# Layer 1 of a graph attention kernel: the sources' attention terms join the products as a 17th column

## The chip, the cores and the metric

The kernel runs on one core of one Trainium2 chip. The metric is the time of one execution on the device in microseconds. Before the change the median of 3 runs was 6350.81 us (6348.14 to 6351.27).

## The reference, cut

Four rounds of message passing over 200,000 edges between 6,250 nodes of 64 channels. Edges are sorted by destination. Three are attention layers (4 heads of 16 channels), the fourth is a linear one. What matters here is the attention layer:

```python
def _gatv2_layer(x, src, dst, Wl, Wr, a, b):
    xl = (x @ Wl).reshape(N, H, O)
    xr = (x @ Wr).reshape(N, H, O)
    s = jax.nn.leaky_relu(xl[src] + xr[dst], NEG_SLOPE)
    e = jnp.einsum('eho,ho->eh', s, a)
    m = jax.ops.segment_max(e, dst, num_segments=N)
    ex = jnp.exp(e - m[dst])
    denom = jax.ops.segment_sum(ex, dst, num_segments=N)
    alpha = ex / (denom[dst] + 1e-16)
    out = jax.ops.segment_sum(xl[src] * alpha[:, :, None], dst, num_segments=N)
    return out.reshape(N, H * O) + b
```

The kernel splits the leaky relu into 0.8 times max(s, 0) and 0.2 times s. The source's share of the second part, 0.2 (xl . a) for each head, is computed once per node and stored as 4 more columns of the table of sources (68 columns, TW). The destination's share is the same for all edges of a node and falls out of the softmax.

## The kernel before

The edges are laid over 128 partitions, 1568 edges in a row on each. A layer works through them in 98 turns of 16 edges a partition (G = 16), two turns to a round of the loop, each with its own buffer (k = 0 or 1). In each turn:

- The 16 source rows of a partition come into `xl[:, k]` (16 rows of 68) in two ways. GpSimd (POOL) issues 12 or 11 indirect DMAs from the table in memory (L552). The other 4 or 5 are fetched by the tensor engine (PE): products of a one-hot matrix with the table held in SBUF (L641), 28 matmuls for each share of 2 columns of edges and 42 for the one of 3. VectorE (DVE) picks the right one of 7 candidate rows with three predicated copies (L1245), and ScalarE (ACT) copies it into `xl` (`rows_copied`).
- DVE's `attention_turn`: the destination rows are spread along runs by a scan (L1284), then the sum `s` (L1307), the product with the positive part `lr` (L1309), the reduction over the 16 channels of a head (L1311), the addition of the source's term (L1312), the running maximum (a scan, L1314), two small operations on the arguments (L1316, L1317), a first select for the next turn, and the weighting `v_g` with the exponential `w_turn` (L1340). After it come the other selects, the one-hot matrix for a later step (layer 1 only, `build_one_hot`, L1233), the scan of the next destination rows, and the four scans of the weighted sums (L1287) with selects between them.
- ACT's `attention_turn`: a copy of the last destination row (`xr_carry`), the exponential `w_turn` (L874) as soon as the arguments are there, the marks for the next turn, the other factors (L858, L859), copies of fetched and of weighted rows, one widening of a one-hot matrix from bf16 (`widen_second`), and, once DVE's last scan of the sums is done (`s_sums`), the carry of the sums (`sums_carry`), the hand-out of the maximum and of the sums (`hand_out_max`, `hand_out`), and the other widening (`widen_first`). Nearly every copy of ACT is recorded with L766, the line of its helper, so groups are told apart by tiles.
- The sync engine (SP) stores the turn (`store_turn`, after `s_out`) and loads marks, indices and one-hot matrices or their codes.

Each engine works in its own written order and waits on semaphores. `done` and `steps_done` count DVE's dependent steps on `s_turn`, `K_TURN` = 5 a turn. `rows_of` gives the count of landed gathers that a turn needs. In layer 1 (`fresh` on ACT, `build` on DVE) the one-hot matrices are built; later layers load them again.

## Time and profile before

| | |
|---|---|
| median of 3 runs | 6350.81 us |
| the profiled execution | 6349.54 us, span 6347.7 us |
| mean granted clock of PE | 0.969 |
| PE busy | 5801.3 us (91%) |
| DVE busy | 5002.1 us (79%) |
| POOL busy | 4666.4 us (74%) |
| ACT busy | 4444.1 us (70%) |

Busy shares are averages over four layers with different limits, so they say little about one of them. Layer 1's loop lies between about 240 and 1670 us of the span, layers 2 and 3 behind it up to about 4750 us, and the linear layer follows. A timeline row has the start, the length, the engine, the line, the operation with its tiles and elements, and, where the engine was idle before it, for how long and what ended that. Neighbours on an engine may overlap by somewhat under 0.1 us, so a start minus the start before is what an instruction takes in a chain.

### The profile page before, as it was taken

The numbers are of one execution on the slowest core, as the hardware profiler recorded it, in microseconds if no ns is written. First come the engines' busy times: TensorE is split into PE (matmuls) and PEld (weight loads), VectorE is DVE, ScalarE is ACT, GpSimd is POOL, SyncE is SP. The second block draws the span as 40 slices with busy tenths as digits, with TensorE's granted clock in tenths as the row PEclk, the third lists the DMA queues.
The fourth block names the chain that finished last, engine by engine and source line by source line (L and its number), as shares of the span: only waits on it lengthen the run. The fifth ranks groups of instructions, "written<-read, shape, count | busy, mean of one in ns | idle before, by whom it ended". The sixth has DMA issues, their size and how long they took to land.

```text
span 6347.7 us, 100679 instructions
## 1 busy us (share of the span) xinstructions
PE 5801.3 (91%) x26479; PEld 4876.6 (77%) x26479; DVE 5002.1 (79%) x7708; ACT 4444.1 (70%) x6153; POOL 4666.4 (74%) x4884
## 2 busy tenths in 40 slices
PE   2899999999799999999969999999986999999996
PEld 1688787787578888888858888888864888888884
DVE  8699999999769999999958999999985444444443
ACT  1588888878468888888837888888874666666663
POOL 3777777777677777777767777777767777777775
PEclk9999999999799999999979999999997999999997
DMA  9677777777445555555535555555553444444442
GB/s 392 228 245 243 242 243 246 243 243 245 136 148 176 178 177 178 177 178 176 178 96 167 178 177 178 177 178 180 177 162 88 146 145 146 146 145 148 146 145 69
DMA packets 453003, 1153.13 MB, mean 182 GB/s; under 512 B 158796, under 2 KB 224832, under 8 KB 416876
## 3 DMA queue, kind: packets, MB, share of 16 engines
q1 hardware_dynamic: 281624, 927.58, 40.5%
q0 software_dynamic: 156944, 173.32, 14.7%
q10 hardware_dynamic: 14404, 51.92, 2.1%
q14 instruction: 24, 0.20, 0.0%
q8 instruction: 7, 0.11, 0.0%
HBM read 754.04 MB, written 398.35 MB: 182 GB/s over the span
## 4 chain that ended last, share of the span: by engine, by line
POOL 41%; issue 20%; PE 13%; DVE 11%; ACT 8%; DMA 3%; SPq 2%; DVEq 1%; POOLq 0%; ACTq 0%
POOL sb_xl L552 36%; PE pG L641 12%; ACT sb_v_in L766 3%; DVE pG L1245 3%; POOL sb_hot_f L552 3%; DVE sb_s_run L1287 2%; ACT sb_hot L766 2%; ACT sb_turn_out L766 2%; DMA sb_xl<-xl_table,sb_idx 2%; POOL marks L556 1%; SPq L364 1%; DVE sb_e_in L1311 1%; DVE sb_lr L1309 1%; DVE sb_s L1307 1%; ACT pB L766 1%
## 5 line engine op out<-in xcount | busy, mean ns | idle before, releaser
L641 PE MATMUL pG<-sb_xl_parts,sb_hot 128*128 128x476 f32 (+1 forms) x25074 | 5507.8, 378 | 221.0 <-ACT sb_xl L766 121.5
L641 PEld LDWEIGHTS pG<-sb_xl_parts,sb_hot 128*128 128x128 f32 x25074 | 4683.2, 189 | 1041.7 <-issue 422.8
L552 POOL DMA_INDIRECT sb_xl<-xl_table,sb_idx x4481 | 4271.2, 953 | 1381.0 <-issue 1352.7
L766 ACT ACTIVATE sb_hot<-sb_wide 128x1792 fp32r<-128x1792 bf16 (+1 forms) x796 | 1485.8, 1880 | 267.1 <-DMA sb_wide<-hots 227.0
L1245 DVE COPY_PREDICATED pG<-sb_pick_turn,pG 128x272 f32<-128x272 int32 (+9 forms) x2388 | 1110.6, 465 | 551.5 <-PE pG L641 455.6
L1287 DVE TENSOR_TENSOR_SCAN sb_s_run<-pB,sb_v_in 128x272 f32<-128x272 f32 (+3 forms) x1470 | 1095.9, 773 | 220.6 <-ACT sb_v_in L999 219.2
L766 ACT ACTIVATE sb_turn_out<-sb_s_run 128x1088 f32<-128x1088 f32 (+2 forms) x399 | 831.9, 2086 | 6.0 <-DVE sb_s_run L1287 6.0
L1284 DVE TENSOR_TENSOR_SCAN pB<-sb_same_c,pB 128x1024 f32<-128x1024 f32 x294 | 672.1, 2286 | 0.2
L766 ACT ACTIVATE sb_xl<-pG 128x136 f32<-128x136 f32 (+4 forms) x838 | 251.6, 303 | 502.6 <-DVE pG L1245 381.9
L766 ACT ACTIVATE sb_v_in<-sb_v_g 128x1024 f32<-128x1024 f32 x291 | 600.7, 2064 | 0.0
L1307 DVE TENSOR_TENSOR sb_s<-sb_xl,pB 128x1024 f32<-128x1024 f32 x294 | 354.5, 1206 | 143.5 <-DMA sb_xl<-xl_table,sb_idx 141.3
L1311 DVE TENSOR_REDUCE sb_e_in<-sb_lr 128x64 f32<-128x1024 f32 x294 | 359.2, 1222 | 10.1
L1309 DVE SCALAR_TENSOR_TENSOR sb_lr<-sb_s,pB 128x1024 f32<-128x1024 f32 x294 | 359.0, 1221 | 10.1
L766 ACT ACTIVATE sb_same_c<-sb_same 128x960 f32 (+1 forms) x294 | 305.7, 1040 | 70.0 <-DVEq L1226 61.9
L1340 DVE TENSOR_TENSOR sb_v_g<-sb_xl,pB 128x1024 f32<-128x1024 f32 x291 | 353.0, 1213 | 0.0
L766 ACT ACTIVATE pB<-sb_mark 128x960 f32<-128x960 f32 x294 | 287.0, 976 | 39.0 <-DMA sb_mark<-marks 21.1
L999 ACT ACTIVATE sb_v_in<-sb_s 128x1024 f32<-128x1024 f32 x97 | 198.9, 2051 | 129.4 <-DVE sb_s L1539 128.1
L766 ACT ACTIVATE sb_v_in<-sb_s_run 128x68 f32<-128x68 f32 (+1 forms) x389 | 126.3, 325 | 189.3 <-DVE sb_s_run L1287 189.3
L874 ACT ACTIVATE pB<-sb_wf_arg 128x64 f32<-128x64 f32 x291 | 65.6, 226 | 245.5 <-DVE sb_wf_arg L1317 242.8
L1539 DVE TENSOR_TENSOR sb_s<-sb_xl,pB 128x1024 f32<-128x1024 f32 x98 | 119.7, 1221 | 138.9 <-DMA sb_xl<-xl_table,sb_idx 119.3
L858 ACT ACTIVATE sb_v_in<-sb_wf_arg 128x64 f32<-128x64 f32 x294 | 75.6, 257 | 168.9 <-DVE sb_v_g L1340 168.9
L556 POOL DMA_INDIRECT marks<-sb_XR,sb_first_edge x147 | 147.0, 1000 | 62.1 <-issue 62.1
(261 smaller groups left out, 2309.4 us busy)
## 6 DMA issues: line engine op xcount, KB each, us to landing
state_rows<-sb_turn_out SPq DMA_DIRECT2D x294, 576.0 KB
sb_wide<-hots SPq DMA_DIRECT2D x149, 1120.0 KB
sb_mark<-marks SPq DMA_DIRECT2D x294, 512.0 KB
sb_wide<-hots SPq DMA_DIRECT2D x149, 896.0 KB
sb_xl<-xl_table,sb_idx POOLq DMA_INDIRECT x4481
sb_wide<-codes SPq DMA_DIRECT2D x50, 1120.0 KB
hots<-sb_wide SPq DMA_DIRECT2D x50, 1120.0 KB, 4.3
marks<-sb_hot_f SPq DMA_DIRECT2D x32, 1568.0 KB
```

The source lines that it names most:

```text
L552: return pool.indirect_dma_start(out=dst, out_offset=None, in_=table, in_offset=bass.IndirectOffsetOnAxis(ap=index, axis=0))
L556: return pool.indirect_dma_start(out=table, out_offset=bass.IndirectOffsetOnAxis(ap=index, axis=0), in_=src, in_offset=None)
L641: product = pe.matmul(pG[:, bank + a - lo, 0:GB * n], hot[k][:, m, a * P:(a + 1) * P], rows[:, :, 0:n], start=(m == 0 and part == 0), stop ...
L766: return act.activation(out, in_, ACT.Copy)
L999: act.activation(v_lin[:, :, 1:G1], s[:].rearrange("p g c -> p c g"), ACT.Relu).then_inc(s_lin_relu, 1)
L1245: return dve.copy_predicated(rows[:, :, 0:n], over(pick_turn[:, k, stage, lo:hi], n), rows[:, :, at:at + n])
L1284: dve.tensor_tensor_scan(xr_flat, same_c[:].rearrange(flat3), xr_flat, 0.0, ALU.mult, ALU.add).then_inc(s_xr, 1)
L1287: return dve.tensor_tensor_scan(s_run[:, lo:hi, :].rearrange(flat3), factors[:, 0:(hi - lo) * G1], v_in[:, lo:hi, :].rearrange(flat3), 0.0 ...
L1307: tt(s[:], xl[:, k, :, 0:C], xr.rearrange("p c g -> p g c"), ALU.add).then_inc(s_added, 1)
L1309: done(dve.scalar_tensor_tensor(out=lr[:], in0=s[:], scalar=0.0, in1=blocks(a_turn, G), op0=ALU.max, op1=ALU.mult)); steps_done()
L1311: done(red(e_turn.rearrange("p h g -> p g h"), lr[:].rearrange("p g (h o) -> p g h o", h=H), AX.X, ALU.add)); steps_done()
L1340: tt(v_g[:].rearrange("p g (h o) -> p g h o", h=H), xl_heads, weights, ALU.mult).then_inc(s_used[k], 1)
```

## The change

In layer 1 the product tile becomes 16 x 4 x 17 values for each partition. The products fill columns 0 to 15 of each head (in all layers), and in layer 1 ACT copies the source's attention term, `xl[:, k, :, C:TW]`, into column 16. DVE's reduction then runs over 17 columns, and its addition L1312 is left out there. ACT copies the terms of a turn ahead, between `hand_out_max` and `hand_out` of the turn before, after it has waited for the gathers and the fetched rows of that turn; the terms of turn 0 are copied ahead of the loop. DVE waits for a new semaphore `s_terms` before the reduction.

```diff
-        lr = sb("lr", [P, G, C])
+        lr_sums = sb("lr", [P, G, H, O + 1])
+        lr = lr_sums[:, :, :, 0:O]
...
+            def attention_terms(landed, copied, k):
+
+                act.wait_ge(s_xl[k], landed)
+                for q in range(2):
+                    act.wait_ge(s_rows[q], copied)
+                copy(lr_sums[:, :, :, O], xl[:, k, :, C:TW]).then_inc(s_terms, 1)
+
...
                     hand_out_max(use * 16, k)
+                    if fresh:
+                        attention_terms(rows_of(l, i + k, 1 - k), selected, 1 - k)
                     hand_out(turn_all + 1, k)
...
                 spread_same(l * TURNS + 1, 1)
+                if fresh:
+                    attention_terms(rows_of(l, 0, 0), l * STEPS + 3, 0)
                 widen_step(4, 0)
...
-                done(dve.scalar_tensor_tensor(out=lr[:], in0=s[:], scalar=0.0, in1=blocks(a_turn, G), op0=ALU.max, op1=ALU.mult)); steps_done()
+                s_heads = s[:].rearrange("p g (h o) -> p g h o", h=H)
+                a_heads = blocks(a_turn.rearrange("p (h o) -> p h o", h=H), G)
+                done(dve.scalar_tensor_tensor(out=lr, in0=s_heads, scalar=0.0, in1=a_heads, op0=ALU.max, op1=ALU.mult)); steps_done()
                 e_turn = e_in[:, 0, :, 1:G1]
-                done(red(e_turn.rearrange("p h g -> p g h"), lr[:].rearrange("p g (h o) -> p g h o", h=H), AX.X, ALU.add)); steps_done()
-                done(tt(e_turn, e_turn, xl[:, k, :, C:TW].rearrange("p g h -> p h g"), ALU.add)); steps_done()
+                e_heads = e_turn.rearrange("p h g -> p g h")
+                if terms:
+                    dve.wait_ge(s_terms, turn_all + 1)
+                    red(e_heads, lr_sums[:, :, :, :], AX.X, ALU.add).then_inc(s_turn, 2)
+                    steps[0] += 2
+                    steps_done()
+                else:
+                    done(red(e_heads, lr, AX.X, ALU.add)); steps_done()
+                    done(tt(e_turn, e_turn, xl[:, k, :, C:TW].rearrange("p g h -> p h g"), ALU.add)); steps_done()
```

`terms` is set in all turns of layer 1 and in no other layer. The prologue's temporary in the same tile is only given its new shape.

## Rows read from the trace of the kernel before

**Rows 1.** Windows, mid layer 1: busy us (xinstructions) of PE, PEld, DVE, ACT, POOL; clock, DMA, GB/s.

```profile
500.00:750.00 250.00, 237.93 (x1075) 200.02 (x1074) 246.46 (x374) 201.38 (x289) 190.30 (x196) 1.00 0.76 244
```

**Rows 2.** Waits of 2000 to 3000 us, layer 2: total us, times, longest.

```profile
DVE sb_s L1307 <- DMA sb_xl<-xl_table,sb_idx: 56.4, 36, 1.8
```

**Rows 3.** DVE's groups, 400 to 1500 us: busy us, mean ns, idle us before.

```profile
L1311 DVE TENSOR_REDUCE sb_e_in<-sb_lr 128x64 f32<-128x1024 f32 x75 | 91.7, 1222 | 2.6
...
L1307 DVE TENSOR_TENSOR sb_s<-sb_xl,pB 128x1024 f32<-128x1024 f32 x74 | 88.0, 1189 | 0.0
...
L1312 DVE TENSOR_TENSOR sb_e_in<-sb_e_in,sb_xl 128x64 f32<-128x64 f32 x75 | 20.6, 275 | 2.6
...
L1316 DVE TENSOR_TENSOR sb_e_in<-sb_m_run,sb_neg_h 128x64 f32<-128x64 f32 x75 | 16.9, 225 | 2.6
```

**Rows 4.** Timeline of DVE, an odd turn of layer 1.

```profile
868.16 1.19 DVE L1307 TENSOR_TENSOR sb_s<-sb_xl,pB 128x1024 f32<-128x1024 f32 x1
...
870.63 1.22 DVE L1311 TENSOR_REDUCE sb_e_in<-sb_lr 128x64 f32<-128x1024 f32 x1
871.89 0.27 DVE L1312 TENSOR_TENSOR sb_e_in<-sb_e_in,sb_xl 128x64 f32<-128x64 f32 x1
872.20 0.30 DVE L1314 TENSOR_TENSOR_SCAN sb_m_run<-sb_neg_h,sb_e_in 128x68 f32<-128x68 f32 x1
...
872.79 0.34 DVE L1317 TENSOR_TENSOR sb_wf_arg<-sb_e_in,sb_m_run 128x128 f32<-128x128 f32 x1
873.13 0.59 DVE L1245 COPY_PREDICATED pG<-sb_pick_turn,pG 128x408 f32<-128x408 int32 x1
873.63 1.21 DVE L1340 TENSOR_TENSOR sb_v_g<-sb_xl,pB 128x1024 f32<-128x1024 f32 x1
...
897.60 1.19 DVE L1307 TENSOR_TENSOR sb_s<-sb_xl,pB 128x1024 f32<-128x1024 f32 x1
```

**Rows 5.** Timeline of ACT in the same turn.

```profile
868.26 0.33 ACT L766 ACTIVATE sb_v_in<-sb_s_run 128x68 f32<-128x68 f32 x1 [0.95 <-DVE sb_s_run L1287]
868.49 0.30 ACT L766 ACTIVATE sb_turn_out<-sb_m_run 128x64 f32<-128x64 f32 x1
868.70 2.17 ACT L766 ACTIVATE sb_turn_out<-sb_s_run 128x1088 f32<-128x1088 f32 x1
870.77 2.44 ACT L766 ACTIVATE sb_hot<-sb_wide 128x2688 fp32r<-128x2688 bf16 x1
873.11 0.21 ACT L766 ACTIVATE sb_xr_carry<-pB 128x64 f32<-128x64 f32 x1
873.21 0.23 ACT L874 ACTIVATE pB<-sb_wf_arg 128x64 f32<-128x64 f32 x1
873.50 0.98 ACT L766 ACTIVATE pB<-sb_mark 128x960 f32<-128x960 f32 x1
874.87 0.26 ACT L858 ACTIVATE sb_v_in<-sb_wf_arg 128x64 f32<-128x64 f32 x1 [0.39 <-DVE sb_v_g L1340]
```

**Rows 6.** Timeline of ACT, the exponential of the even turn behind it.

```profile
887.55 0.23 ACT L874 ACTIVATE pB<-sb_wf_arg 128x64 f32<-128x64 f32 x1 [0.61 <-DVE sb_wf_arg L1317]
```

**Rows 7.** Timeline of ACT and DVE in the last turn of layer 1.

```profile
1666.09 0.23 ACT L874 ACTIVATE pG<-sb_wf_arg 128x64 f32<-128x64 f32 x1 [2.31 <-DVE sb_wf_arg L1317]
...
1666.35 1.98 DVE L1323 TENSOR_TENSOR sb_v_in<-sb_xl,pG 128x1024 f32<-128x1024 f32 x1 [0.29 <-ACT pG L874]
```

**Rows 8.** Timeline of POOL and DVE beside the one-hot build.

```profile
875.31 1.59 POOL L552 DMA_INDIRECT sb_xl<-xl_table,sb_idx  x1 [0.30 <-issue]
...
876.03 0.75 DVE L1233 TENSOR_SCALAR sb_wide<-sb_wide,sb_code_no 128x2048 bf16<-128x2048 int16 x1
...
877.21 0.94 POOL L552 DMA_INDIRECT sb_xl<-xl_table,sb_idx  x1 [0.30 <-issue]
```

**Rows 9.** Timeline of PE in the same turn.

```profile
876.59 21.82 PE L641 MATMUL pG<-sb_xl_parts,sb_hot 128*128 128x476 f32 x98 [1.20 <-ACT sb_xl L766]
```

**Rows 10.** Timeline of DVE near the end of layer 1.

```profile
1657.46 0.59 DVE L1245 COPY_PREDICATED pG<-sb_pick_turn,pG 128x408 f32<-128x408 int32 x1 [0.58 <-PE pG L641]
```

More of the change, by code:

```diff
@@ L216, in build @@
         pe_src = s[0:STEPS].rearrange("p g c -> p (g c)")[:, 0:ECX].bitcast(I32)
-        pe_tmp = lr[0:STEPS].rearrange("p g c -> p (g c)")[:, 0:ECX]
+        pe_tmp = lr_sums[0:STEPS].rearrange("p g h o -> p (g h o)")[:, 0:ECX]
         out_flat = turn_out[:].rearrange("p k g r -> p (k g r)")
@@ L298, in build @@
         s_e_carried = sem("max_carried")
+        s_terms = sem("attention_terms_in")
         s_sums, s_out, s_stored = sem("sums_scanned"), sem("turn_out_ready"), two("turn_stored")
@@ L1295, in linear_sums, with attention_turn @@
                 scan_sums(same_part, LIN_SUMS[-2], LIN_SUMS[-1]).then_inc(s_sums, 1)
-            def attention_turn(l, i, k, last=False, build=False):
+            def attention_turn(l, i, k, last=False, build=False, terms=False):
                 use = l * PAIRS + i
@@ L1393, in attention_layer @@
                     for k in range(2):
-                        attention_turn(l, i, k, build=build)
-                attention_turn(l, PAIRS - 2, 0, build=build)
-                attention_turn(l, PAIRS - 2, 1)
-                attention_turn(l, PAIRS - 1, 0)
-                attention_turn(l, PAIRS - 1, 1, last=True)
+                        attention_turn(l, i, k, build=build, terms=build)
+                attention_turn(l, PAIRS - 2, 0, build=build, terms=build)
+                attention_turn(l, PAIRS - 2, 1, terms=build)
+                attention_turn(l, PAIRS - 1, 0, terms=build)
+                attention_turn(l, PAIRS - 1, 1, last=True, terms=build)
                 dve.wait_ge(s_sums, (l + 1) * TURNS)
```

## The prediction, made before the change was built

> **What bounds the kernel now.** I read the busy time by stretches first, then the groups of instructions of layer 1's loop, then the timelines of VectorE (DVE) and ScalarE (ACT) over one pair of turns side by side. In a stretch in the middle of layer 1 DVE is busy 246.46 of 250 us [rows 1], and the sum of sources and destinations, which starts each turn, waited for nothing in 74 turns (idle 0.0) [rows 3]. So DVE sets the pace there: two turns take 29.44 us (868.16 to 897.60, the starts of two sums of the same parity) [rows 4]. In layers 2 and 3 the same sum waits for the gathers of sb_xl, 36 times in 1000 us and up to 1.8 us each [rows 2]: they pace that loop, and DVE's length is hidden there. The change touches the work of layer 1 alone, except for the pitch of sb_lr, below.
>
> The two turns of a pair are not alike, and this decides the case. Call a turn odd when ACT has just widened the large share of the one-hot matrix (2688 columns, 2.44 us), and even when it was the small one. In the odd turn at 868.16 follow both engines from one event, the end of the last scan of the sums. DVE goes sum, product, reduction (870.63), the addition (871.89), the running maximum (872.20), arguments (872.79), a select (873.13), and at 873.63 the weighting sb_v_g, which needs ACT's exponential [rows 4]. ACT goes carry (868.26), maximum (868.49), hand-out (868.70), widening (870.77), xr_carry (873.11), exponential, 873.21 to 873.44 [rows 5]. In this chain ACT has no gap at all: its idle time of 0.95 us is before the carry, and the exponential follows xr_carry at once. From 873.44 to the weighting's start are 0.19 us; of these 0.03 go to the hand-over (ACT's exponential ends at 1666.32, DVE's product starts at 1666.35 [rows 7]). So ACT is only 0.16 us ahead of being the later of the two. In the even turn ACT waited 0.61 us for the arguments before the same exponential [rows 6]; there it has room.
>
> **Part 1: the addition goes.** It takes 275 ns [rows 3], and from its start to the start of the running maximum it is 0.31 us (871.89 to 872.20) [rows 4]. That is what goes, the gap that follows each dependent step included.
>
> **Part 2: the reduction reads 17 columns.** 1088 elements in place of 1024. Between an operation of 64 elements (225 ns) and the one of 1024 (1222 ns) an element costs 997/960 = 1.04 ns [rows 3], so 64 more cost 0.07 us. DVE's own chain becomes shorter by 0.31 - 0.07 = 0.24 us in each turn. Its additional wait for the terms costs nothing: the copy comes 0.44 us after ACT's carry starts and the reduction 2.47 us after the sum starts [rows 4, 5], and the running maximum, which already waits for two semaphores (`steps_done` and `s_e_carried`), shows the same 0.04 us gap (872.16 to 872.20) as the addition that waits for one (871.85 to 871.89) [rows 4].
>
> **Part 3: ACT's copy.** No row shows it: 64 elements in runs of four, read from SBUF at a pitch of 68 and written at a pitch of 17. It stands between the maximum's copy and the hand-out, so it pushes back the hand-out, the widening, xr_carry and the exponential. What matters is its step, from its start to the start of what follows. From below: the exponential of 64 elements into sb_v_in takes 0.26 us, less the 0.09 by which neighbours overlap (868.49 + 0.30 against 868.70) is 0.17; I take 0.16 to 0.17. The copy of the maximum, also 64 elements and read at a pitch of 17, has a step of 0.21, and the carry, scattered on both sides, 0.23 [rows 5]. From above: the copy has three waits and a register to work out, and the copy of the marks starts 0.29 us after the exponential before it (873.21 to 873.50), although that lasts 0.23, for it has such waits in front [rows 5]; so 0.30. A step below nothing is excluded, since ACT works in order. I take 0.22, nearest to the two scattered copies, with 0.16 and 0.30 as ends.
> The wait for the gathers that is put in front of the copy would hold up the hand-out, its store, the widening for TensorE (PE) and the exponential. It is the wait that DVE's next sum has too, and that sum starts at 868.16, before the carry, never having waited for gathers [rows 3]; so it costs nothing. ScalarE's widening ends near 873.2 and PE begins the following share at 876.59, after a wait for another copy [rows 9]; 0.22 us more are hidden there by some 3 us. SP's queue gets its store 0.22 us later in a period of 14 us, and ACT waits for that store only two turns later. If that cover went, each 0.1 us would cost 0.1 us a turn.
> The Trainium skill's page "ScalarE: Activation LUTs", section "What ACT_TABLE_LOAD costs", gives 186 ns plus 0.833 ns an element for such an ACTIVATE, and 93 ns of overlap of neighbours. An estimate by that page is 239 ns and a step of 0.15 us. The trace has 0.30 us and a step of 0.21 for 64 scattered elements [rows 5], so here the row speaks against it.
>
> **The sum.** Even turns: ACT's exponential could run 0.61 us before it did; with the copy 0.39, and DVE's arguments come 0.24 earlier. DVE still comes last, so the whole 0.24 is won. Odd turns: DVE would be ready for the weighting 0.24 us earlier, but ACT's exponential comes 0.22 later and had 0.16 to spare: the weighting starts 0.22 - 0.16 = 0.06 us later than now. The gain turns into a wait for ACT. Of 49 even turns the one next to the layer's end wins nothing, because DVE waits 0.58 us for PE behind it [rows 10]: 48 x 0.24 = 11.5 us won. Of 49 odd turns the last one has no widening before it and wins 0.24; the other 48 lose 48 x 0.06 = 2.9. Together 11.5 + 0.2 - 2.9 = 8.8 us won. The profiled execution took 6349.54 us, so 6340.7; the median of the runs shown lies 1.3 us above that execution, which makes 6342.0 us. With a step of 0.16 odd turns neither win nor lose: 11.7 us, 6339.1. With 0.30 they lose 48 x 0.14 = 6.7: 5.0 us won, 6345.8.
> What else could come last at this pace: GpSimd (POOL). Its gathers follow each other at 1.24 us [rows 8] and there are 23 in a pair, 28.5 us, plus one that took 1.59 in place of 0.94, 29.2. That looks almost like a bound at today's 29.44, but the long one (875.31 to 876.90) ends 0.12 us after the one-hot build that DVE runs from 876.03 to 876.78 [rows 8]: it is held by that build and shrinks when POOL comes later relative to DVE. Its 0.65 us are room, more than the 0.18 us by which the pair shortens. PE idles 1.20 us a pair [rows 9].
>
> **The rivals.** (a) *Both turns win.* Then 97 x 0.24 = 23.3 us, 6327.5. It needs the weighting at 873.39, while ACT's exponential already ends at 873.44 before the change [rows 4, 5]; only a chain of ACT that I misread allows it. 4%.
> (b) *A cheap copy.* ACT's exponential into PSUM, 64 elements too, takes 0.23 us [rows 5], a step of 0.14. With that odd turns win 0.02: 12.7 us, 6338.1, and a little less or 0.02 more slack is over 0.2%. That contiguous row speaks for it, both scattered ones against. 14%. By the Trainium skill's page "ScalarE: Activation LUTs", section "What ACT_TABLE_LOAD costs", it would be this case.
> (c) *ACT becomes the bound of both turns: slower.* Beyond a step of 0.37 (0.61 less 0.24) even turns wait for ACT as well, and a pair changes by (step - 0.16) + (step - 0.61). That is nothing at a step of 0.385; from 0.52 it is slower by over 0.2%; at 0.60 it is +0.43 a pair, 21 us, 6372. For it: three waits on one instruction, in a queue that has no gap. Against it: 0.29 is the longest such step in the rows. 8%.
> (d) *The pitch of 17 slows DVE.* DVE's product into sb_v_in, all of it scattered, took 1.98 us, against 1.21 for the same product into rows [rows 4, 7]. sb_lr is now written in runs of 16, and read so in layers 2 and 3. If a run costs one element more, 64 x 1.04 = 0.07 us, even turns win 0.17, odd ones don't notice, and it is 5.5 us won, 6345.3; if it cost the whole 0.77 us in each turn it would be some 50 us slower. The 225 ns step reads runs of 16 at a pitch of 17 and shows nothing of it. 6%, of which 1 slower.
> (e) *POOL falls into a build twice in a pair*, another 0.65 us: its period would be 28.5 + 1.3 = 29.8, DVE would come to wait for gathers, and 49 pairs would take 49 x 0.36 = 18 us more than now, 6368. It holds only if the new phase keeps hitting. 4%.
>
> **How the numbers follow.** The forecast has 64%: 6342.0, of its own range 6339 to 6346. A measurement of this kernel can tell some 0.2% (12.7 us) from no change, that is below 6338.1 or above 6363.5. Faster: (a), and two thirds of (b), 13%. Slower: most of (c), half of (e), the worst of (d), 9%. Within: 78%. The range holds 8 in 10 from 6336.5 ((b), with the 1.5 us by which runs scatter) to 6350 (mild (d) and the first half of (c)).
>
> **What would show it.** In the profile after: no 64-element addition in layer 1; a reduction of 1088 elements at 1.29 us; a copy from sb_xl to sb_lr on ACT, with its step; in odd turns a wait of the weighting for ACT's exponential of some 0.2 to 0.3 us, in even turns none, and an idle time before the even exponential of some 0.15 us; a pair of 29.26 us; layers 2 and 3 unchanged. I am wrong if the odd turn's weighting doesn't wait, if the copy's step lies outside 0.14 to 0.30, or if sb_lr's product takes other than 1.22 us.

## The result and the profile after

The changed kernel takes 6358.1 us (median of 20 runs) against 6349.8 us for the kernel before (20 runs): a ratio of 1.0014, 95% interval 1.0008 to 1.0020, or 8.3 us more. The forecast was 6342.0 us, 7.8 us less, and the time lies outside its range. That is 0.13%, less than the 0.2% that the prediction took as the least change one can tell, but the interval excludes no change at all, and the direction is the opposite of the forecast's. One of the 20 runs (6850.9 us, with a mean granted clock of 0.803 in place of 0.969) was a slow one and is left out of the ratio.

| | before | after |
|---|---|---|
| profiled execution (span) | 6349.54 (6347.7) us | 6369.94 (6368.1) us |
| a pair of turns in layer 1, from sum to sum | 29.45 us | 29.65 us |
| odd turn, even turn | 14.38, 15.06 us | 14.38, 15.26 us |
| layer 1, first sum to last | 1426.3 us | 1434.9 us |
| layers 2, 3 and 4 | 1391.6, 1390.8, 1395.1 us | 1395.8, 1394.8, 1397.6 us |

A pair of turns is one round of the loop. The profiled execution of after is 11.8 us above its own median. Its gathers (the indirect DMAs that POOL issues) lasted 0.947 us in place of 0.944; some 3360 gathers in layers 2 to 4 by 0.003 us are 10 us, and these three layers together are 10.7 us longer. That is a matter of this execution and not of the change: e2 below has the same pitch of sb_lr there, and gathers of 0.944 us, and its layers 2 to 4 take 1390.9, 1391.4 and 1394.6 us. The profiled executions of e1 and e3 are of the same kind as after's, that of g8 is not, and its layer 1 is as long (1434.4 us). What makes the gathers of an execution longer isn't known. The timed difference of 8.3 us is layer 1's 8.6.

Windows in the middle of layer 1, after, answering to [rows 1]:

```profile
500.00:750.00 250.00, 236.73 (x1067) 198.76 (x1066) 244.72 (x353) 202.00 (x304) 190.75 (x194) 1.00 0.76 242
```

VectorE (DVE) is busy for 1.7 us less of 250, yet a pair takes 0.20 us longer. Its groups of 400 to 1500 us, after, answering to [rows 3] (busy us, mean ns, idle us before):

```profile
L1329 DVE TENSOR_REDUCE sb_e_in<-sb_lr 128x64 f32<-128x1088 f32 x75 | 96.6, 1288 | 6.7
...
L1324 DVE SCALAR_TENSOR_TENSOR sb_lr<-sb_s,pB 128x1024 f32<-128x1024 f32 x75 | 91.6, 1222 | 2.6
...
L1320 DVE TENSOR_TENSOR sb_s<-sb_xl,pB 128x1024 f32<-128x1024 f32 x74 | 88.0, 1190 | 0.0
...
L1246 DVE TENSOR_SCALAR sb_wide<-sb_wide,sb_code_no 128x2560 bf16<-128x2560 int16 x37 | 39.7, 1072 | 0.0
...
L1246 DVE TENSOR_SCALAR sb_wide<-sb_wide,sb_code_no 128x1920 bf16<-128x1920 int16 x37 | 34.5, 932 | 0.0
```

The same two builds of the one-hot matrix in the same view of the kernel before:

```profile
L1233 DVE TENSOR_SCALAR sb_wide<-sb_wide,sb_code_no 128x2560 bf16<-128x2560 int16 x37 | 33.0, 892 | 0.0
...
L1233 DVE TENSOR_SCALAR sb_wide<-sb_wide,sb_code_no 128x1920 bf16<-128x1920 int16 x37 | 26.4, 712 | 0.0
```

The addition is gone, the reduction takes 1288 ns, the product still 1222. But two instructions that the change doesn't touch grew by 0.18 and 0.22 us in each pair: the two builds of the even turn. Here they are in the timeline of DVE, after, a pair of turns from 872.11 us (odd) and 886.49 us (even), answering to [rows 4]:

```profile
872.11 1.19 DVE L1320 TENSOR_TENSOR sb_s<-sb_xl,pB 128x1024 f32<-128x1024 f32 x1
...
877.57 1.22 DVE L1362 TENSOR_TENSOR sb_v_g<-sb_xl,pB 128x1024 f32<-128x1024 f32 x1
...
879.99 0.75 DVE L1246 TENSOR_SCALAR sb_wide<-sb_wide,sb_code_no 128x2048 bf16<-128x2048 int16 x1
...
886.49 1.19 DVE L1320 TENSOR_TENSOR sb_s<-sb_xl,pB 128x1024 f32<-128x1024 f32 x1
887.71 1.22 DVE L1324 SCALAR_TENSOR_TENSOR sb_lr<-sb_s,pB 128x1024 f32<-128x1024 f32 x1
889.02 1.29 DVE L1329 TENSOR_REDUCE sb_e_in<-sb_lr 128x64 f32<-128x1088 f32 x1
890.35 0.30 DVE L1336 TENSOR_TENSOR_SCAN sb_m_run<-sb_neg_h,sb_e_in 128x68 f32<-128x68 f32 x1
...
891.99 1.21 DVE L1362 TENSOR_TENSOR sb_v_g<-sb_xl,pB 128x1024 f32<-128x1024 f32 x1
...
893.61 0.92 DVE L1246 TENSOR_SCALAR sb_wide<-sb_wide,sb_code_no 128x1920 bf16<-128x1920 int16 x1
...
894.91 1.07 DVE L1246 TENSOR_SCALAR sb_wide<-sb_wide,sb_code_no 128x2560 bf16<-128x2560 int16 x1
```

ScalarE (ACT) in the same pair, answering to [rows 5, 6]; in brackets its idle time and what ended it:

```profile
872.65 0.30 ACT L768 ACTIVATE sb_lr<-sb_xl 128x64 f32<-128x64 f32 x1
872.80 2.17 ACT L768 ACTIVATE sb_turn_out<-sb_s_run 128x1088 f32<-128x1088 f32 x1
...
877.32 0.22 ACT L883 ACTIVATE pB<-sb_wf_arg 128x64 f32<-128x64 f32 x1
...
891.27 0.23 ACT L883 ACTIVATE pB<-sb_wf_arg 128x64 f32<-128x64 f32 x1 [0.20 <-DVE sb_wf_arg L1339]
```

GpSimd (POOL), answering to [rows 8]:

```profile
878.74 1.05 POOL L554 DMA_INDIRECT sb_xl<-xl_table,sb_idx  x1 [0.30 <-issue]
880.09 1.46 POOL L554 DMA_INDIRECT sb_xl<-xl_table,sb_idx  x1 [0.30 <-issue]
...
893.10 0.95 POOL L554 DMA_INDIRECT sb_xl<-xl_table,sb_idx  x1 [0.30 <-issue]
894.35 0.98 POOL L554 DMA_INDIRECT sb_xl<-xl_table,sb_idx  x1 [0.30 <-issue]
895.64 1.16 POOL L554 DMA_INDIRECT sb_xl<-xl_table,sb_idx  x1 [0.30 <-issue]
```

Read the even turn against these. Its weighting starts 5.50 us after its sum (before: 888.23 - 882.54 = 5.69), so 0.19 us are won, as meant. Then both builds start about half a microsecond into a gather (893.61 against 893.10, 894.91 against 894.35) and last 0.92 and 1.07 us. That gives 0.21 and 0.18 us back, and the turn ends 0.20 us later than before. In the odd turn the weighting starts 5.46 us after the sum, against 5.47: it waits for ACT's exponential, which ends at 877.54.

In the kernel before, the even turn's builds met the gathers at other points. DVE's two builds and POOL's gathers beside them:

```profile
889.85 0.71 DVE L1233 TENSOR_SCALAR sb_wide<-sb_wide,sb_code_no 128x1920 bf16<-128x1920 int16 x1
...
890.95 0.89 DVE L1233 TENSOR_SCALAR sb_wide<-sb_wide,sb_code_no 128x2560 bf16<-128x2560 int16 x1
```

```profile
888.44 0.94 POOL L552 DMA_INDIRECT sb_xl<-xl_table,sb_idx  x1 [0.30 <-issue]
889.69 0.98 POOL L552 DMA_INDIRECT sb_xl<-xl_table,sb_idx  x1 [0.30 <-DVE sb_v_g L1340]
890.98 0.98 POOL L552 DMA_INDIRECT sb_xl<-xl_table,sb_idx  x1 [0.30 <-issue]
```

They started 0.16 and 1.26 us after the start of the latest gather, and kept their length. The first two even turns of layer 1 in the changed kernel still take 14.87 and 14.90 us, with short builds; from the third on they take 15.27. How the loop gets from the one to the other is shown under e4.

### The profile page after: what moved, and what is told of

Same layout as the page of the kernel before. It is cut to its first block, busy times and chain, and to the rows that moved or that the text cites. A ratio compares the mean times of both kernels' runs of the same rounds, so it can differ in the third digit from the quotient of the medians.

```text
span 6368.1 us, 100875 instructions
## 1 busy us (share of the span) xinstructions
PE 5809.6 (91%) x26479; PEld 4875.3 (77%) x26479; DVE 5000.5 (79%) x7610; ACT 4461.9 (70%) x6251; POOL 4687.0 (74%) x4884
## 4 chain that ended last, share of the span: by engine, by line
POOL 48%; issue 23%; DVE 10%; ACT 8%; DMA 4%; PE 3%; SPq 2%; DVEq 1%; POOLq 0%; ACTq 0%
POOL sb_xl L554 43%; ACT sb_v_in L768 3%; DVE pG L1258 3%; POOL sb_hot_f L554 3%; PE pG L643 3%; DMA sb_xl<-xl_table,sb_idx 2%; ACT sb_hot L768 2%; DVE sb_s_run L1300 2%; ACT sb_turn_out L768 2%; POOL marks L558 1%; SPq L366 1%; DVE sb_lr L1324 1%; DMA sb_idx<-src_edges 1%; DVE sb_s L1320 1%; DVE sb_e_in L1329 1%
## 5 line engine op out<-in xcount | busy, mean ns | idle before, releaser
L1333 DVE TENSOR_REDUCE sb_e_in<-sb_lr 128x64 f32<-128x1024 f32 x196 | 239.4, 1222 | 6.7
```

The costliest lines, as they stand in the source:

```text
L1333: done(red(e_heads, lr, AX.X, ALU.add)); steps_done()
```

## The experiments

The theory formed from the two traces: a build on DVE and a gather on POOL hold each other up, and the shortened turn moved the builds onto the bad part of the gathers. The rivals: ACT's copy on the path of the odd turn's exponential, the pitch of 17, and the additional wait.

### The halves of the change, and more work added

**e1_after_again** is the changed kernel once more, beside the next three.

> The changed kernel once more, as the measure for the others of this group. Meeting theory (the shorter even turn moves the two builds of the one-hot matrix in it to where a gather of GpSimd is at work, and both engines then hold each other up; the loop settles there): a pair of turns of 29.6 us, in even turns builds of 0.93 and 1.07 us in place of 0.71 and 0.89, some 8 us slower than before. Rival (the 12 us that the first profile of the changed kernel has outside layer 1 belong to the change): layers 2 to 4 again 4, 4 and 3 us longer than before and a time near 6370.

Measured: 6356.85 us against 6348.15 (33 runs of the kernel before), 1.0011 (1.0002 to 1.0020); a pair of 29.64 us, the even turn's builds 0.93 and 1.07 us. It repeats.

**e2_copy_alone**: ACT copies the terms, DVE computes as before.

```diff
-                    dve.wait_ge(s_terms, turn_all + 1)
-                    red(e_heads, lr_sums[:, :, :, :], AX.X, ALU.add).then_inc(s_turn, 2)
...
+                    done(red(e_heads, lr, AX.X, ALU.add)); steps_done()
+                    done(tt(e_turn, e_turn, xl[:, k, :, C:TW].rearrange("p g h -> p h g"), ALU.add)); steps_done()
```

> Only ScalarE's part: it copies the terms into column 16 with all its waits, while VectorE sums 16 columns and adds the terms itself as before. Meeting theory: VectorE's turns keep their length (the copy's step of 0.15 us fits into ScalarE's 0.16 us of room in odd turns), so the builds stay where they were: a pair of 29.45 us and the time of before within 2 us. Rival (ScalarE's later hand-out and exponentials cost the time): 8 us slower than before, as the whole change is.

Measured: 6350.64 us, 1.0001 (0.9992 to 1.0010), and a pair of 29.45 us. Its builds, 400 to 1500 us:

```profile
L1246 DVE TENSOR_SCALAR sb_wide<-sb_wide,sb_code_no 128x2560 bf16<-128x2560 int16 x37 | 33.0, 893 | 0.0
...
L1246 DVE TENSOR_SCALAR sb_wide<-sb_wide,sb_code_no 128x1920 bf16<-128x1920 int16 x37 | 26.4, 713 | 0.0
```

The copy and the pitch of 17 cost nothing by themselves. DVE's shortening is needed for the loss.

**e3_dve_alone**: 17 columns on DVE, no copy on ACT. Column 16 is set to zero once, so the sources' terms are left out of the sums.

```diff
-                    if fresh:
-                        attention_terms(rows_of(l, i + k, 1 - k), selected, 1 - k)
...
-                    dve.wait_ge(s_terms, turn_all + 1)
...
+                if build:
+                    dve.memset(lr_sums[:, :, :, O], 0.0)
```

> Only VectorE's part: it reduces 17 columns and has no addition, column 16 is zeroed once ahead of the loop, ScalarE copies nothing and VectorE doesn't wait for it. The sources' attention terms are left out of layer 1. Meeting theory: even turns are 0.24 us shorter up to the weighting, so the builds meet the gathers as in the changed kernel, and it is no faster than before (6350 to 6362) with builds of over 0.9 us in even turns. Rival (ScalarE's part eats the gain): 18 to 22 us faster than before, 6328 to 6332, builds of 0.71 and 0.89 us.

Measured: 6349.12 us, 1.0000 (0.9991 to 1.0009). Without the copy the odd turn is 14.22 us, 0.16 shorter than in the changed kernel: that is the copy's step of 0.15 on ACT's path. The even turn is 15.27 us, as long as in the changed kernel, with the same long builds:

```profile
L1242 DVE TENSOR_SCALAR sb_wide<-sb_wide,sb_code_no 128x2560 bf16<-128x2560 int16 x37 | 39.6, 1071 | 0.0
...
L1242 DVE TENSOR_SCALAR sb_wide<-sb_wide,sb_code_no 128x1920 bf16<-128x1920 int16 x37 | 33.9, 917 | 0.0
```

By the prediction's sum this kernel should have won 0.24 us in each even turn and, with no copy on ACT, its 0.16 us of room in each odd one, 19 us in all. The odd turns won their 0.16 and the even turns lost 0.20, so nothing was won, with ACT's copy out of the case. This also settles the gap of 0.09 us ahead of the long reduction (888.93 to 889.02 in the trace of after; 0.04 before): it is 0.10 here, where no additional wait stands in front (883.56 + 1.22 against 884.88). So it belongs to the reduction over 17 columns, not to the wait. e2, which keeps the pitch of 17 and reduces 16 columns, has the same idle total of 2.6 us before the reduction as [rows 3], against 6.7 in after.

**e4_phase_back**: the changed kernel plus a useless product of 240 elements on DVE behind the even turn's reduction, which puts that turn's later work back to where it was.

```diff
+        pad = sb("pad", [P, 4, 60])
...
+                    if k == 0:
+                        tt(pad[:, :, :], s[:, 0:4, 0:60], blocks(a_turn[:, 0:60], 4), ALU.mult)
```

> The changed kernel with an idle VectorE product of 240 elements (result unused, one source in PSUM) behind the reduction of even turns, which puts the builds back by some 0.2 us to where they stood before the change. Meeting theory: more work and less time: a pair of 29.43 us, builds of 0.71 and 0.89 us, some 9 us faster than the changed kernel, that is the time of before within 2 us. Rival (the time goes elsewhere): 49 x 0.2 = 10 us slower than the changed kernel, 6368.

Measured: 6349.42 us, 0.9999 (0.9990 to 1.0008). With more work on DVE than e1 it is 7.4 us faster, and 9 of e1's 11 runs are above all 11 of e4. The pad doesn't bring a gain over the kernel before, but it takes the loss away. Its single runs spread from 6344.2 to 6355.7 us, and the profiled one (6355.7) shows why. DVE's two builds of the even turn in layer 1, first from 240 to 830 us and then from 860 to 1600 us of the same execution:

```profile
L1247 DVE TENSOR_SCALAR sb_wide<-sb_wide,sb_code_no 128x2560 bf16<-128x2560 int16 x20 | 17.8, 892 | 0.0
...
L1247 DVE TENSOR_SCALAR sb_wide<-sb_wide,sb_code_no 128x1920 bf16<-128x1920 int16 x20 | 14.2, 712 | 0.0
```

```profile
L1247 DVE TENSOR_SCALAR sb_wide<-sb_wide,sb_code_no 128x2560 bf16<-128x2560 int16 x25 | 26.8, 1071 | 0.0
...
L1247 DVE TENSOR_SCALAR sb_wide<-sb_wide,sb_code_no 128x1920 bf16<-128x1920 int16 x25 | 19.3, 771 | 0.0
```

For 21 pairs the loop runs at 29.41 to 29.45 us with short builds. At 833 us it slips once, and every pair from 854 us on takes 29.65 to 29.68 us. The instructions are the same in both halves; only where the builds fall in the gathers differs. What POOL waited for before and after the slip, from 300 to 820 us and from 860 to 1600 us (us, times, longest), shows what slipped:

```profile
POOL sb_xl L555 <- issue: 118.6, 389, 0.3
POOL sb_xl L555 <- DVE sb_v_g L1365: 5.5, 18, 0.3
```

```profile
POOL sb_xl L555 <- issue: 175.3, 575, 0.3
```

Before the slip one gather of nearly every pair is released by DVE's weighting, which frees the buffer; the kernel before has 45 such between 300 and 1600 us (889.69 above is one). After the slip none is, as in the changed kernel: POOL has fallen 0.7 us behind DVE (the sum started 0.34 us after the start of a gather, and starts 0.89 us after that of the gather before it).

The trace shows the slip itself, in the even turn from 824.49 us:

```profile
832.90 0.88 DVE L1247 TENSOR_SCALAR sb_wide<-sb_wide,sb_code_no 128x2560 bf16<-128x2560 int16 x1
```

```profile
833.05 1.55 POOL L555 DMA_INDIRECT sb_xl<-xl_table,sb_idx  x1 [0.30 <-issue]
```

Before, the second build of the even turn started 0.03 us ahead of a gather, which then lasted 0.98 us (803.48 and 803.51 us here; 890.95 and 890.98 above). Here it starts 0.15 us ahead, because one earlier gather (829.18) had lasted 1.06 us, and the gather waits: 1.55 us. From the next pair on the builds are long. In the changed kernel the same happens in the second even turn, and there the shortened turn itself brings the build so far ahead:

```profile
272.57 0.88 DVE L1246 TENSOR_SCALAR sb_wide<-sb_wide,sb_code_no 128x2560 bf16<-128x2560 int16 x1
```

```profile
272.73 1.52 POOL L554 DMA_INDIRECT sb_xl<-xl_table,sb_idx  x1 [0.30 <-issue]
```

In the 14 traces named below, the gathers that start up to 0.06 us behind a build's start are held up by 0.03 us (116 gathers), those that start 0.10 to 0.22 us behind it by 0.54 (461). What holds the loop there afterwards is the first build. In after, e1, e3, e4 and g8 it starts anywhere from 0.48 to 0.66 us into its gather, and it always ends 1.42 to 1.44 us after that gather's start (207 builds). So what DVE does ahead of it may come up to 0.2 us sooner or later, and DVE goes on behind it at the same time against the gather. That is why e4's pad, once the loop has slipped, costs only 0.02 us a turn (15.29 against 15.27).

And POOL never pauses in either state. Its gathers follow each other at 1.249 us, 23 of them are 28.73 us, and with the time by which they are held up (0.72 us a pair in the kernel before, 0.70 and 0.94 in e4 before and behind the slip, 0.91 in g8 below) that is 29.45, 29.43, 29.67 and 29.64 us: the pairs' lengths within 0.01. (These sums say no more than that POOL never pauses; they don't say which engine holds up the other.) In e3 the sum comes out too (0.76 with that execution's longer gathers, 29.49), and the even builds are long, though one gather a pair is still released by the weighting. It is another one, in the odd turn (before the slip it is in the even turn), and POOL lags there as in the changed kernel: the sums start 0.88 us after the start of a gather.

**g8_even_only**: only the even turns get the change. ACT copies their terms in idle time ahead of the sums, so that the copy is on nobody's path, and the wait stands ahead of the sum.

```diff
+                    if fresh and k == 1:
+                        attention_terms(rows_of(l, i + k, 1 - k), selected, 1 - k)
...
+                terms = terms and k == 0
+                if terms:
+                    dve.wait_ge(s_terms, use + 1)
```

> Only the turns with the small widening (even ones) get the change; the others keep the kernel before's addition and reduction, and the wait for the terms stands ahead of the even turn's sum, where ACT has copied them in idle time. By the prediction's sum this is all gain: 48 even turns by 0.24 to 0.30 us, nothing lost in odd turns, a pair of 29.17 to 29.21 us in place of 29.45 and 12 to 14 us off the whole, some 6336. By the theory of the builds (a one-hot build of VectorE that begins 0.45 to 0.7 us after a gather's start on GpSimd takes 0.2 us longer, and the gather up to 0.5 us longer) the shortened even turn moves its own two builds against the gathers: they come out at 0.9 and 1.07 us in place of 0.71 and 0.89, the pair at 29.4 to 29.6 us and the whole at 6348 to 6357. The rival that ACT's copy on the path to the odd exponential costs the time expects the first figures, for the copy is on no path here. If the builds' starts happen to lie off 0.45 to 0.7 us, the builds keep their length and the first figures come out as well: then the loss is a matter of phase alone, which the builds' lengths in the trace would show.

Measured: 6359.92 us against 6350.79, 1.0015 (1.0006 to 1.0024), 9.1 us slower. The odd turn is 14.38 us as before, the even one 15.25, the pair 29.63. Its builds, 400 to 1500 us:

```profile
L1246 DVE TENSOR_SCALAR sb_wide<-sb_wide,sb_code_no 128x2560 bf16<-128x2560 int16 x37 | 39.6, 1071 | 0.0
L1246 DVE TENSOR_SCALAR sb_wide<-sb_wide,sb_code_no 128x1920 bf16<-128x1920 int16 x37 | 33.0, 891 | 0.0
```

By the prediction this half was the whole gain, 11.5 us. It is the whole loss.

### Runs in which TensorE set the pace

The next kernels ran where TensorE was granted less (mean clock 0.86 in place of 0.97) and layer 1's pair took 39 to 40 us, with DVE waiting for TensorE's rows. Their times say nothing of the loop that DVE and POOL set, but their traces say where builds and gathers meet.

**e5_plain_ops, f5_plain_ops, g5_plain_ops**: the changed kernel, with the four builds replaced by reductions of about the same lengths, so that the loop of layer 1 builds no one-hot matrices and the fetched rows are wrong; the codes that the matrices are built from are shifted too.

```diff
-                        ins = ts(pe_codes[m // 3][:, m % 3 * ECX:(m % 3 + 1) * ECX], tmp, -(ROUND + m), None, ALU.add)
+                        ins = ts(pe_codes[m // 3][:, m % 3 * ECX:(m % 3 + 1) * ECX], tmp, -(ROUND + m - 16), None, ALU.add)
...
-                        build_one_hot(1 - k, 0, BUILD_FIRST)
+                        stand_in(*((0, 9, 59), (16, 7, 62))[k])
...
-                        build_one_hot(1 - k, BUILD_FIRST, GB).then_inc(s_hot[1 - k], 1)
+                        stand_in(*((32, 11, 64), (48, 9, 63))[k]).then_inc(s_hot[1 - k], 1)
```

> The changed kernel, in whose loop of layer 1 each of the two builds of the one-hot matrix is replaced by a reduction of float32 values of the same length (0.61, 0.75, 0.71, 0.89 us): the same VectorE time, but no fast mode on 16-bit data. No one-hot matrices are built in the loop, so the rows fetched by TensorE are wrong. Meeting theory: these operations and the gathers don't hold each other up: no gather over 1.0 us in layer 1, a pair of 29.25 us, layer 1 some 10 us shorter than before and 19 us shorter than in the changed kernel, 6338 to 6342. Rival (the pair is long for another reason than the builds' mode, such as the waits or the pitch of 17): a pair of 29.6 us and 6357.

> The same kernel as e5_plain_ops, on another chip: that one let TensorE run so slowly (before took 8659 us there) that TensorE set the pace of all layers and VectorE's turns didn't show. Meeting theory (builds of the one-hot matrix and gathers hold each other up): with reductions of the same length in place of the builds no gather over 1.0 us in layer 1, a pair of 29.25 us, 6338 to 6342. Rival: a pair of 29.6 us and 6357.

> The same kernel as e5_plain_ops once more; the chips of e5 to f8 ran TensorE so slowly that it set the pace of every layer. Meeting theory: without builds in the fast mode no gather over 1.0 us in layer 1, VectorE's operations keep their lengths, a pair of 29.25 us, 6338 to 6342. Rival: a pair of 29.6 us and 6357.

**e6_terms_early, f6_terms_early**: the changed kernel with all terms copied ahead of the sums. **e7_early_build_first, e8_early_build_second**: the same with both builds of a turn in one place, the first or the second. **f7_odd_only, f8_even_only**: its halves (f8 is the kernel of g8_even_only).

> The changed kernel with the copy of the terms moved ahead of ScalarE's wait for the last scan of the sums, into its 0.95 us of idle time there, and VectorE's wait for it moved ahead of its sum. Both turns' own chains are shorter than in the changed kernel (odd 0.15, even 0.05 us). Meeting theory: GpSimd with its stalls (23 x 1.25 + 0.7 us) is the bound then, as with VectorE's part alone: a pair of 29.4 to 29.5 us, 6347 to 6351, better than the changed kernel and no better than before. Rival (ScalarE's chain set the time): VectorE wins 0.4 us a pair, 29.05 us, 6330.

> The same kernel as e6_terms_early, on another chip for the same reason: the terms are copied in ScalarE's idle time. Meeting theory: a pair of 29.4 to 29.5 us, 6347 to 6351, no better than before. Rival (ScalarE's chain set the time): 29.05 us, 6330.

> As e6_terms_early, with the build in one piece at the place of the first part. Meeting theory: one long operation of 1.1 to 1.3 us in place of two; whichever gather it meets, there is one stall a turn and not two, but a longer one: between 29.2 and 29.6 us a pair, and its gathers' and builds' lengths must add up to it. Rival (builds don't matter): the same time as e6_terms_early within 2 us.

> As e7_early_build_first, with the one piece at the place of the second part, behind the last select of the first share. It moves the build against the turn by some 0.3 us and saves the wait for ScalarE's copy by nothing. Meeting theory: the builds of both turns move together, so the gathers meet them as in e7_early_build_first, and the time is the same within 3 us. Rival (the place in the turn matters, because selects and the copy of rows come later): slower than e7_early_build_first by more.

> As f6_terms_early, but only odd turns sum 17 columns; even turns add the terms as before. From the odd turn's builds to the even turn's builds nothing changes against before, so meeting theory says that the gathers stay where they were: builds of 0.71 and 0.89 us in even turns, odd turns 0.17 us shorter, a pair of 29.27 us, 8 us faster than before, 6340 to 6342. Rival (GpSimd's work alone is the bound near 29.45 us, wherever its stalls come from): the time of before.

> The reverse: only even turns sum 17 columns, odd ones add as before. VectorE's own work is 0.24 us a pair less than before, about as in f7_odd_only. Meeting theory: the even turn's builds come earlier against the gathers, as in the changed kernel: builds of over 0.9 and 1.0 us there, a pair of 29.6 us, 6355 to 6359. Rival (the turn in which the work goes doesn't matter): the same as f7_odd_only within 2 us.

Measured, as ratios to the kernel before on the same chip (8659.3, 8632.9 and 8649.2 us): e5 1.0028 (1.0016 to 1.0040), e6 1.0016 (1.0003 to 1.0028), e7 1.0048 (1.0032 to 1.0064), e8 1.0036 (1.0021 to 1.0052); f5 1.0033 (1.0020 to 1.0047), f6 1.0013 (0.9996 to 1.0030), f7 1.0011 (0.9997 to 1.0025), f8 1.0015 (1.0005 to 1.0026); g5 1.0043 (1.0027 to 1.0059). As times they settle nothing: where an expectation names a pair near 29 us it was not tested. e7 is 29 us slower than e6, where its rival said within 2 us, and its gathers are held up by 1.27 us a pair against 0.64; e8 is 8 us from e7, with single runs that spread over more than that. What they do tell stands in the lengths. Gathers and stand-ins of e5 from 400 to 2000 us:

```profile
L555 POOL DMA_INDIRECT sb_xl<-xl_table,sb_idx x924 | 873.3, 945 | 727.5 <-DVE sb_v_g L1363 470.5 <-issue 256.9
...
L1368 DVE TENSOR_REDUCE sb_pad<-sb_s 128x11 f32<-128x704 f32 x41 | 36.0, 878 | 0.0
```

and gathers and the longest build of e6 in the same stretch:

```profile
L554 POOL DMA_INDIRECT sb_xl<-xl_table,sb_idx x936 | 909.7, 972 | 691.4 <-DVE sb_v_g L1363 431.1 <-issue 260.3
...
L1246 DVE TENSOR_SCALAR sb_wide<-sb_wide,sb_code_no 128x2560 bf16<-128x2560 int16 x41 | 44.1, 1075 | 0.0
```

With reductions in the builds' place no gather is held up (945 ns on average, as where nothing stands beside them). With builds the mean gather is 972 ns, and the build of 892 ns takes 1075.

**h1_before_half, h2_after_half, h3_plain_half, h4_odd_half**: the kernels before, after, e5 and f7 with TensorE's matmuls over the second part of the table's values left out, to get DVE to set the pace again.

```diff
-                        for part in range(PARTS):
+                        for part in range(1):
...
```

> The kernel before with half of TensorE's fetching: only the high parts of the table are multiplied, so fetched rows lack their low bits. TensorE can then not set the pace, even on a chip that slows it. It is the measure for the next three, and VectorE, ScalarE and GpSimd have all their work. All theories: a pair of 29.45 us in layer 1 and 28.75 in layers 2 and 3, even turns with builds of 0.71 and 0.89 us, one gather of 1.59 us a pair.

> The changed kernel with the same half of the fetching. Meeting theory: a pair of 29.6 us in layer 1, builds of 0.93 and 1.07 us in even turns, some 9 us slower than h1_before_half. Rival (TensorE has a part in the loss, by selects that come later): a pair of 29.2 us and 10 us faster than h1_before_half.

> As h2_after_half, with ordinary reductions of the same length in place of the fast builds in the loop (the kernel of e5_plain_ops; no one-hot matrices are built there). Meeting theory: no gather over 1.0 us in layer 1, a pair of 29.25 us, some 19 us faster than h2_after_half and 10 faster than h1_before_half. Rival (the loss is not in the mode of the builds): the time of h2_after_half.

> As h2_after_half, but with the terms only in odd turns and their copy in ScalarE's idle time (the kernel of f7_odd_only). Meeting theory: the way from the odd turn's builds to the even turn's is as before, so even turns keep builds of 0.71 and 0.89 us, odd turns are 0.17 us shorter: a pair of 29.27 us, 8 us faster than h1_before_half. Rival (GpSimd is the bound at 29.45 us): the time of h1_before_half.

Measured: 8492.1, 8499.8, 8840.7 and 8501.0 us (before on this chip 8647.8). TensorE's clock fell further, to 0.72, the pairs of layer 1 still took about 37 us, and 44 in h3. The aim was missed, and the times tell nothing of the case. That h3 was 341 us slower than h2, where 19 us faster was expected, is not explained; its odd turns took 29.6 us in place of 20.6. One thing h1 does show: it is the kernel before but for the matmuls left out, and at this other pace its longer even build lasts 1.08 us and not 0.89. A long build is a matter of where it falls, and not of the change.

### Where the builds fall, over all traces

From the traces of the 14 kernels that keep the four builds (before, after, e1 to e4, g8, e6, f6 to f8, h1, h2, h4) I took for each build of layer 1's loop the time from the start of the latest gather to its own start, and by how much it was longer than its usual length:

| build starts after the gather's start | builds | longer by, mean |
|---|---|---|
| up to 0.45 us | 669 | 0.00 us |
| 0.45 to 0.55 us | 182 | 0.20 us |
| 0.55 to 0.65 us | 538 | 0.18 us |
| 0.65 to 0.75 us | 142 | 0.01 us |
| over 0.75 us | 1129 | 0.00 us |

All but two of the 720 builds that began 0.45 to 0.65 us into a gather are the even turn's (1920 and 2560 columns); the two of 2048 columns kept their length. The even turn's builds that began elsewhere kept theirs too, but for a few: 0.06 us at most in the rows outside 0.45 to 0.75.

The gathers beside a build lasted 1.15 us on average (2546 gathers, 1787 of them over 1.0 us), the others 0.946 (12930, of which 28 over 1.0). With stand-ins (e5, f5, g5, h3) 200 reductions began 0.45 to 0.65 us after a gather's start and kept their usual length (0.00 us); 615 gathers beside stand-ins lasted 0.944 us, none over 1.0. So both sides pay, DVE only if it comes into a certain part of the gather, and it is the build, a `tensor_scalar` on 16-bit values, that does it, not any DVE work. Which of its two properties, the instruction or the 16 bits, no run tells.

The Trainium skill's page "SBUF — State Buffer", section "Who interferes with whom", says that DVE's two-port modes, which `tensor_scalar` can enter, share a pair of ports with GpSimd under a lock, and that `tensor_reduce` never contends on this chip. The runs agree on both kinds of instruction. By the same section whoever comes second "fully blocks" until the other's instruction is over. That fits the gather of 1.59 us in the kernel before, which ends 0.12 us after its build [rows 8]. The builds disagree: one that begins earlier than 0.45 us into a gather isn't held up at all, and one that begins 0.5 us into a gather of 0.95 is held up by 0.2 us and not by 0.45. If a lock is what holds them up, the gather doesn't have it for its whole length; no run shows the lock itself.

## Why the prediction was wrong

**What held.** None of the signs that the prediction had named for its being wrong came true; they all look at DVE and ACT, and none at POOL. The reduction of 1088 elements at 1.29 us; the product at 1.22 us at the new pitch, so rival (d) is out; no wait for gathers or for TensorE at the copy; in the odd turn a wait of the weighting for ACT (0.68 us from the select's start to it, where it was 0.50 [rows 4]); an idle time of 0.20 us before the even exponential, where some 0.15 was forecast. ACT remains ahead in even turns, and (c) didn't come about.

**Terms that were mis-sized.** The copy's step is 0.15 us (872.65 to 872.80), below the 0.16 to 0.30 given; the copy itself lasts 0.30 us, as the scattered ones do, but what follows starts sooner. That was rival (b). The odd turn therefore wins 0.01 us in place of losing 0.06. The estimate worked out from the page "ScalarE: Activation LUTs" of the Trainium skill, 0.15, was right on the step, though not on the copy's length (0.24 against 0.30 us), and the choice of the rows against it was wrong. In the even turn 0.19 us are won up to the weighting, not 0.24, for the gap ahead of the reduction over 17 columns is 0.05 us longer, a cost that the sum didn't have. With these two terms alone the time would have come out at 48 x 0.19 + 48 x 0.01 = 9.6 us won, near the forecast. (The 1.3 us by which the median was taken to lie above the profiled execution is 0.2 with the 20 runs.)

**The step that failed** is the last one of the sum, on POOL: "Its 0.65 us are room". Two things are wrong in it. First, the period. The working took 1.24 us for the step of a gather and got 28.5 us for 23; the rows of the trace step by 1.249 (877.21 [rows 8] to 888.44, above, are nine steps of 1.248), so it is 28.73. With the long gather's 0.65 and the 0.07 of the two gathers of 0.98 beside the even builds it is 29.45, today's pair to the hundredth. POOL had no room at all, and that it never pauses could be read before the change, from its waits: one gather a pair was released by the weighting, after the same 0.30 us as all others. Second, the stretch of a gather was taken as something that happens to POOL alone and shrinks as POOL comes later. A meeting also lengthens DVE's build, by 0.2 us, and the sum took the builds' lengths as fixed. So when DVE's even turn became 0.19 us shorter, its second even build came to start 0.16 us ahead of a gather in place of 0.03, that gather was held up by 0.57 us in place of 0.03, POOL, already at its limit, fell 0.7 us behind, and from the third pair on the even builds fell into the bad part of the gathers, where both loops stay: 0.19 won, 0.39 lost, 0.20 x 46 pairs = 9 us slower.

Rival (e) had the place, POOL falling into builds more often, and the sign, but at 4%, with 0.65 us a meeting on POOL's side and none on DVE's, so 6368 us. DVE does not come to wait for gathers, as that rival had it; its builds get longer instead. Its price was too high, for in the new state the gathers are held up by 0.91 us a pair (g8) in place of 0.72, and its chance was far too low: e1, e3, g8 and the larger part of e4's trace all settle at long even builds.

**What stays open.** What in a gather holds up a build, and why only in that part of it, isn't shown; nor why the one gather ahead of e4's slip lasted 1.06 us, so that other executions of e4 may slip earlier, later or not at all. The stand-ins and the odd turns alone (f7) were not had at the pace of 29 us a pair, so that a kernel without the meetings would win the time back is argued and not measured, and no kernel here beats the kernel before. The changed kernel's first two pairs took 29.24 and 29.25 us, 0.20 less than before; if the loop could be kept from slipping it would be that over the whole layer, by an estimate some 9 us.

## What to carry to other kernels

When two engines both run without a pause in the same loop, work out the period of each from its own rows to the hundredth: where both equal the loop's, shortening one of them isn't a gain until something is found that the other gives up too. Ahead of a change that moves a 16-bit `tensor_scalar` on VectorE against indirect DMAs on GpSimd, write down at which point of a gather each one starts now and will start then, for here a shift of 0.13 us, from 0.03 to 0.16 us ahead of a gather, was enough to cost more than leaving out an instruction of 64 elements brought. A loss that vanishes when useless work is added speaks for phase, that is for where two engines' instructions meet, and padding is a cheap way to find out.

## What the runs showed of the hardware

- A 16-bit build on DVE that starts 0.45 to 0.65 us after the start of an indirect DMA on POOL takes some 0.2 us longer (720 builds, mean 0.19, all but two of 0.71 and 0.89 us); up to 0.45 and from 0.75 us on, 0.06 at most. The gather beside it takes up to 1.6 us in place of 0.944.
- The build of 0.71 us, when it is held up, ends 1.42 to 1.44 us after the gather's start, wherever from 0.48 to 0.66 us it started (207 builds in five traces). Two loops are tied to each other that way.
- A gather that starts up to 0.06 us behind a build's start is held up by 0.03 us (116 gathers), one that starts 0.10 to 0.22 us behind it by 0.54 on average (461).
- One execution can hold two paces of the same loop: 29.43 and then 29.67 us a pair (e4), each steady over 20 pairs and more.
- A copy of 64 scattered elements on ACT lasts 0.30 us and holds up what follows by 0.15.
- A reduction over 17 columns on DVE starts 0.05 us later behind its producer than one over 16.
- In some executions (the profiled ones of after, e1 and e3 among them) nearly every undisturbed gather lasts 0.947 us in place of 0.944, and in these three layers 2 to 4 together are 8 to 11 us longer; not explained.
